# Moving the order of matmuls in the even groups of a decay mix with a routed low-rank layer

## What is computed

```python
ekv_t, ek_t = exp(min(f, 30)) * f, exp(min(f, 30))
# forward and backward over time: a = a * decay + ekv_t ; b = b * decay + ek_t
num = nf + nb - ekv + exp(min(u + f, 30)) * f
den = df + db - ek + exp(min(u + f, 30))
y = sigmoid(x) * num / max(den, 1e-8) * (0.8 + 0.2 * tf)
```

```python
h = silu(y @ rw1.T + rb1)                      # 64 hidden
logits = (h @ rw2.T + rb2)[:, :16] + gates     # top 2, softmax of the two -> coeff
xa = einsum('ni,eri->ner', y, A)               # 256 low-rank sums for a token
out = x + y @ W.T + bias + einsum('ner,eor->no', xa * coeff[:, :, None], B)
```

## Time and profile before

| | |
|---|---|
| median of 3 runs | 720.68 us (720.63 to 720.79) |
| the profiled execution: its time, its span | 720.62 us, 718.8 us |
| PE busy | 597.5 us (83%) |
| PEld busy | 486.8 us (68%) |
| DVE busy | 528.0 us (73%) |
| ACT busy | 349.3 us (49%) |
| POOL busy | 352.2 us (49%) |
| DMA | 74.22 MB, mean 103 GB/s |

### The profile page before, as it was taken

The page is one execution under the profiler, slowest core; times in us unless marked ns, Lnnn a source line. Parts: engine busy times, 40 slices in busy tenths (PEclk is TensorE's granted clock), DMA queues, the critical chain, the costliest instruction groups (busy, mean ns, idle before and its releaser), DMA issues.

```text
span 718.8 us, 6928 instructions
## 1 busy us (share of the span) xinstructions
PE 597.5 (83%) x2626; PEld 486.8 (68%) x2626; DVE 528.0 (73%) x547; ACT 349.3 (49%) x401; POOL 352.2 (49%) x164
## 2 busy tenths in 40 slices
PE   0005342498999999999999999999999999999998
PEld 0003231386888688868886888778887888888886
DVE  7999999799788979796979796979698713021302
ACT  4777876845574556435664565356735420002000
POOL 1789988744754575356536553655464511000100
PEclk9999665599999999999999999999999999999999
DMA  5324442313350435041613261226214310231031
GB/s 181 117 86 143 141 142 88 118 59 117 127 167 30 146 103 191 29 147 59 224 41 120 86 208 56 74 104 209 83 50 138 95 55 1 88 110 38 0 89 73
DMA packets 30865, 74.22 MB, mean 103 GB/s; under 512 B 4464, under 2 KB 4592, under 8 KB 30832
## 3 DMA queue, kind: packets, MB, share of 16 engines
q1 hardware_dynamic: 30832, 73.79, 30.8%
HBM read 57.00 MB, written 16.78 MB: 103 GB/s over the span
## 4 chain that ended last, share of the span: by engine, by line
PE 59%; DVE 16%; POOL 16%; issue 6%; ACT 2%; DMA 0%; DVEq 0%; SPq 0%; POOLq 0%; ACTq 0%
PE acc L707 18%; PE acc L708 18%; PE acc L709 18%; POOL mix L461 5%; DVE mix L534 4%; DVE yr L560 3%; POOL kv L451 3%; POOL yr L456 3%; POOL y_lo L465 2%; POOL wx_lo L471 2%; DVE mix L539 2%; DVE xo L567 2%; PE acc L719 2%; PE acc L718 2%; ACT y_hi L314 1%
## 5 line engine op out<-in xcount | busy, mean ns | idle before, releaser
L707 PE MATMUL acc<-y_hi,wa_hi 128*128 128x512 f32 x640 | 257.3, 402 | 10.5 <-DVE xo L567 10.5
L708 PE MATMUL acc<-y_lo,wa_hi 128*128 128x512 f32 x640 | 253.5, 396 | 0.0
L709 PE MATMUL acc<-y_hi,wa_lo 128*128 128x512 f32 x640 | 253.2, 396 | 0.0
L707 PEld LDWEIGHTS acc<-y_hi,wa_hi 128*128 128x128 f32 x640 | 123.0, 192 | 43.6 <-DVE xo L567 18.2
L709 PEld LDWEIGHTS acc<-y_hi,wa_lo 128*128 128x128 f32 x640 | 122.7, 192 | 26.4
L708 PEld LDWEIGHTS acc<-y_lo,wa_hi 128*128 128x128 f32 x640 | 123.0, 192 | 24.9
L461 POOL TENSOR_TENSOR mix<-mix,kv 128x1024 f32<-128x1024 f32 x31 | 74.1, 2390 | 90.6 <-DVE mix L518 73.7
L718 PE MATMUL acc<-y_hi,wr 128*128 128x512 f32 x64 | 27.3, 426 | 99.3 <-POOL wa_lo L439 63.6
L567 DVE SCALAR_TENSOR_TENSOR xo<-acc,bias_sb,xo 128x512 f32<-128x512 f32 x64 | 46.7, 736 | 76.5 <-PE acc L709 76.4
L465 POOL TENSOR_TENSOR y_lo<-yr,y_hi 128x1024 fp32r<-128x1024 f32 x32 | 76.6, 2395 | 49.9 <-ACT y_hi L314 49.9
L471 POOL TENSOR_TENSOR wx_lo<-xa,wx_hi 128x512 fp32r<-128x512 f32 x16 | 20.4, 1298 | 152.6 <-ACT wx_hi L373 152.6
(11 more groups left out here) (85 smaller groups left out, 767.4 us busy)
## 6 DMA issues: line engine op xcount, KB each, us to landing
kv<-f_cm SPq DMA_DIRECT2D x32, 512.0 KB, 3.3
yr<-x_cm SPq DMA_DIRECT2D x32, 512.0 KB, 3.3
xo<-x_cm SPq DMA_DIRECT2D x64, 256.0 KB, 4.0
out<-xo SPq DMA_DIRECT2D x64, 256.0 KB, 3.5
xo<-w_base SPq DMA_DIRECT2D x5, 512.0 KB, 3.5
xa<-w_base SPq DMA_DIRECT2D x3, 512.0 KB, 4.3
xa<-w_router_a SPq DMA_DIRECT2D x2, 480.0 KB, 3.4
xo<-w_expert SPq DMA_DIRECT2D x1, 512.0 KB, 3.8
```

Of the source, the lines that this page charges most:

```text
L707: nc.tensor.matmul(out_ap, wh, yh, start=start, stop=False)
L708: nc.tensor.matmul(out_ap, wh, yl, start=False, stop=False)
L709: return nc.tensor.matmul(out_ap, wl, yh, start=False, stop=stop)
```

## The change

In the even groups, TensorE goes over the channel blocks in the outermost loop: for each kc the router, both low-rank sums, and, three units behind (LAG), base block 0. Base block 1 comes ahead of the logits, base block 2 between logits and spreads, behind a wait for the first low-rank copy, and the last three units of block 0 behind the spreads. `bank_in` waits for the evacuation that frees a bank, just ahead of the first matmul into it. Group 0's waits for weights are joined into one for each kc. Odd groups keep their order; only the way in which the waits are written is new. No instruction is added or removed but waits, and no other engine's order is touched.

```diff
--- before.py
+++ after.py
@@ -760,46 +760,62 @@
                 if G % 2 == 0:
                     pe.wait_ge(lo_ready, G // 2 * CB + kc + 1)
 
+            def bank_in(G, n):
+                if G:
+                    pe.wait_ge(evacuated, (G - 1) * CB + 4 + n)
+
             for G in range(GROUPS):
-                if G == 0:
+                LAG = 3
+                if G % 2 == 0:
                     for kc in range(CB):
                         unit_in(G, kc)
-                        pe.wait_ge(w_lo_ready, router_a_chunk[kc] + 1)
+                        if G == 0:
+                            pe.wait_ge(w_lo_ready, max(router_a_chunk[kc], base_chunk[kc]) + 1)
+                        if kc == 0:
+                            bank_in(G, 0)
                         hid(G, kc)
-                        low_rank(G, 0, kc)
-                        low_rank(G, 1, kc)
-                        pe.wait_ge(w_lo_ready, base_chunk[kc] + 1)
+                        for a in range(2):
+                            if kc == 0:
+                                bank_in(G, 1 + a)
+                            low_rank(G, a, kc)
+                        if kc >= LAG:
+                            if kc == LAG:
+                                bank_in(G, 3)
+                            base(G, 0, kc - LAG)
+                    bank_in(G, 4)
+                    for kc in range(CB):
+                        base(G, 1, kc)
+                    if G == 0:
+                        pe.wait_ge(late_in, 16 * 7)
+                    logits(G)
+                    pe.wait_ge(xa_copied, 2 * G + 1)
+                    for kc in range(CB):
+                        base(G, 2, kc)
+                    pe.wait_ge(xa_copied, 2 * G + 2)
+                    for a in range(2):
+                        spread(G, a)
+                    for kc in range(CB - LAG, CB):
                         base(G, 0, kc)
-                    pe.wait_ge(late_in, 16 * 7)
                 else:
-                    first = 5 if G % 2 == 0 else CB
-                    pe.wait_ge(evacuated, (G - 1) * CB + 4)
-                    for kc in range(first):
-                        unit_in(G, kc)
+                    bank_in(G, 0)
+                    for kc in range(CB):
                         hid(G, kc)
                     for a in range(2):
-                        pe.wait_ge(evacuated, (G - 1) * CB + 5 + a)
-                        for kc in range(first):
+                        bank_in(G, 1 + a)
+                        for kc in range(CB):
                             low_rank(G, a, kc)
-                    for kc in range(first, CB):
-                        unit_in(G, kc)
-                        hid(G, kc)
-                    for a in range(2):
-                        for kc in range(first, CB):
-                            low_rank(G, a, kc)
-                    pe.wait_ge(evacuated, (G - 1) * CB + 7)
+                    bank_in(G, 3)
                     for kc in range(CB):
                         base(G, 0, kc)
-                logits(G)
-                if G:
-                    pe.wait_ge(evacuated, G * CB)
-                for kc in range(CB):
-                    base(G, 1, kc)
-                pe.wait_ge(xa_copied, 2 * G + 2)
-                for a in range(2):
-                    spread(G, a)
-                for kc in range(CB):
-                    base(G, 2, kc)
+                    logits(G)
+                    bank_in(G, 4)
+                    for kc in range(CB):
+                        base(G, 1, kc)
+                    pe.wait_ge(xa_copied, 2 * G + 2)
+                    for a in range(2):
+                        spread(G, a)
+                    for kc in range(CB):
+                        base(G, 2, kc)
                 for a in range(2):
                     pe.wait_ge(wx_ready, 2 * G + a + 1)
                     for kc in range(2):
```

## The result

The changed kernel took 732.24 us (median of 4 runs, 730.4 to 734.37), the kernel before 720.68 (720.63 to 720.79). The ratio is 1.0161, 95% interval 1.0129 to 1.0193: slower by 11.6 us. The runs of before lie within 0.2 us, those of the changed kernel within 4. The profiled execution took 730.4 us, its span is 728.6: 9.8 us over the one of before.

A forecast was written before the change was run, and what follows sets the result against it. Bound: a loop of TensorE's work from block 5 to logits plus DVE's stretch from logits to evacuations. 0.6 (group 0) + 0.5 (clock, block 2) + 2 x 3.41 (late logits) + 3 x 0.5 (clock, block 5) = 9.4: 730.1 us, range 726.0 to 733.5.

The forecast's parts named there:

- rival A: The forecast: late logits are paid for in groups 2 and 4, with some clock falls, 727.5 to 732.5 us; chance 0.65.
- B: Rival: every gap brings TensorE's clock to half, each at its full price, 732.5 to 735.5 us; chance 0.16.
- full price: Most that half clock costs behind a gap: 1.45 us ahead of block 5, 2.75 us ahead of group 0's block 2.
- the lateness of group 0: In group 0, spreads, DVE's second weighing, the evacuation and block 5 come 0.6 us later.
- Logits 15 matmuls later: Groups 2 and 4: DVE's routing and evacuations move with the logits, costing 3.41 us each, 6.8 together; group 6 costs 0.
- The late router sum: Group 2: sum read at 289.1 instead of 283.92, hidden vector still 1.9 us ahead of logits; cost 0.
- covering the 4.67 us: Group 0: block 1 fills TensorE's 4.67 us of idleness before logits; DVE gains nothing, 3.3 us of waiting ahead of block 5.
- The clock: Half clock at new gaps: 0.5 us ahead of group 0's block 2, 0.5 at each of three ahead of block 5.
- the 0.5 us ahead of block 2: Group 0: clock cost of the 2.85 us gap ahead of block 2, between 0 and 2.75 us, taken as 0.5.
- C: Rival: DVE's 19.26 us from routing to evacuation shrink by 1 to 2 in groups 2 and 4, 724.0 to 727.5; chance 0.12.
- D: Rival: the first evacuation follows TensorE's results, not routing; groups 2 and 4 lose nothing, 718.0 us; chance 0.04.
- E: Rival: DVE's waiting and idleness absorb all but 0.4 of the 3.41 us, nothing measurable, 720 to 722 us; chance 0.03.

The follow-up runs named there:

- e12: The changed kernel with its four new gaps filled by 55 matmuls that nobody needs: 727.48 us.
- e3: The kernel before with only the logits of groups 2, 4 and 6 moved 15 matmuls later, inside base block 1: 731.06 us.
- e7: The changed kernel with logits of groups 2, 4 and 6 back behind 88 matmuls and spreads 24 matmuls behind them: 727.47 us.
- e6: The changed kernel with units of blocks 3 and 4 moved ahead of block 5, four in even groups and two in odd ones: 720.04 us.
- e9: e1 with the last three units of group 0's block 0 right behind its logits, ahead of the wait for the low-rank copy: 721.72 us.
- e1: The new order in group 0 alone, groups 1 to 7 as in the kernel before: 724.43 us.
- e2: The new order in groups 2, 4 and 6 alone, the other groups as in the kernel before: 728.94 us.
- e5: The kernel before with two more units of blocks 3 and 4 (12 matmuls) moved ahead of block 5 in every group: 708.62 us.
- e10: e9 with units of blocks 3 and 4 moved ahead of block 5, two in groups 1 to 7, all six in group 0: 709.01 us.
- e11: e10 with logits six matmuls earlier in groups 1 to 7 and spreads 24 matmuls behind them: 708.34 us.

## Why the prediction was right

It said 730.1 us, 726.0 to 733.5, slower; 732.24 were measured. The main mechanism, rival A's, is what the traces show. Part of B holds as well: the clock went to half around all four new gaps, though in the median not at B's full price. That the shortest execution took 730.4 us, next to the forecast, is luck: the median is 2.1 us over it, since the lateness of group 0 was put 0.5 us too high and the clock 2.8 too low, and the longest run, 734.37, lies outside the range, in B's.

**Logits 15 matmuls later, 3.41 us in each of groups 2 and 4, nothing in group 6.** Shown. The gap ahead of block 5 is 3.74 us, DVE's stretch kept its length to 0.03 us, group 6's reserve shrank by 3.41; e12 has 6.9 us for lateness in all, where 6.8 were counted for these groups; and e3 moves block 5 by 3.44 us with the position of the logits alone.

**The late router sum at no cost.** Right for this kernel: read at 289.2 where 289.1 was said, wait for logits 0.83 where 0.8 was said. e7 and e6 show how near it was: with logits at their old place it costs 2.6 us a group, with the gaps filled it bounds the kernel.

**Group 0: covering the 4.67 us gains nothing.** Right, routing began at 143.28. The 0.6 us of lateness was too much, and the gap ahead of block 5 is 2.69 us, not 3.3. In the changed kernel block 5 comes 1.70 us late (166.88 against 165.18), but nearly all of that is block 2 at half clock. In e12, where spreads came at 151.79 as said and the next scan behind the weighing 0.75 us late, block 5 is only 0.1 late (group 1's logits at 218.70 against 218.62): an operation of DVE in between was shorter by 0.65, see below.

**The clock.** The mechanism was right and the size was off: 2.0 us were counted (0.5 and three times 0.5), and the medians give 4.8, single runs 2.9 to 6.9. The term that failed first is the 0.5 us ahead of block 2, taken as small because its gap was thought to be the shortest. It is the dearest in the medians, since nothing hides the slow matmuls there and DVE waits for the spreads behind them: e9, whose gap there is 1.21 us where e1 has 3.93, is 2.7 us faster than e1. Behind block 5 of group 0 the price changes most. By how much later than block 5 the logits of group 1 are, it is 0.03 us in the profile of the changed kernel, 1.75 in that of e1 and 1.95 in that of e9; 0.5 was counted and 1.45 given as the most. Behind block 5 of groups 2 and 4, e2 has 728.94 - 720.67 - 6.82 = 1.5 us for both, 0.7 each against 0.5. The slow block 5 hid there, as said: the second gap, 1.19 us, is gone in these groups, and so the statement that it would stay was wrong. Mostly for this reason the waits for evacuations came to 15.7 us and not to about 20.

**The Trainium skill's rule.** By the Trainium skill (TensorE: Matmul & The Clock Gate, HAM oscillation) bursts of matmuls between long enough waits are throttled again at every one of them. The profiled execution agrees: the clock went to half around each of its four new gaps (3.03, 2.69, 3.74 and 3.73 us). The full price of the four, by the prediction's own bounds, is 2.75 + 3 x 1.45 = 7.1 us. The median paid 4.8, the shortest run 2.9, the longest 6.9. The prediction calls the full price 3.9 us more than it counts; its own terms give 7.1 - 2.0 = 5.1.

C, D and E are out: nothing in the 19 us shrank, and the evacuation did not follow TensorE's results.

## What to carry to other kernels

When an engine's work is handed over in a loop (matmuls, then a fixed stretch of another engine, then matmuls that need it), count what stands ahead of the handover and what stands beside the other engine's stretch; moving work from the first to the second is worth the gap that it closes (e5 moved 2.7 us a group, closed gaps of 1.7 to 1.9 and gained 12.0 in all), and the other way costs its length where no reserve takes it up (3.41 us in groups 2 and 4, nothing in group 6), though the work stays the same. It ends where the other engine becomes the bound (e10, e11). Filling an idle stretch ahead of a handover gains nothing if the receiver wasn't waiting (group 0). A gap in TensorE's work can cost more than its length, by the half clock behind it, where nothing hides what comes behind it (2.7 us between e1 and e9): put real work there, or split the work around it.

## What the runs showed of the hardware

Behind group 0's logits, the granted clock was at half in or behind every gap of 2.1 us or more that the profiles show: 2.10 and 2.17 us in e6, 2.20 and 2.21 in e3, 2.69 to 3.74 in the changed kernel, 2.88 in e10, 3.93 in e1. Around most gaps of 1.2 to 1.8 us it stayed full, but not around all: e6 has it at half behind its gap of 2.10 us, which ended at 346.27, and e7 behind one of 1.45 us, which ended at 447.82, though not behind one of 1.46 us at 296.10. The stretches are first of e6, then of e7 (columns as in the earlier trace rows):

```profile
346.30:347.00 0.70, 0.70 (x3) 0.61 (x4) 0.70 (x2) 0.70 (x1) 0.70 (x1) 1.00 0.00 0
347.20:350.40 3.20, 3.20 (x9) 2.52 (x8) 3.20 (x3) 0.30 (x1) 3.12 (x2) 0.50 0.92 264
```

```profile
447.90:449.20 1.30, 1.30 (x10) 1.23 (x11) 1.30 (x1) 1.28 (x2) 1.22 (x2) 1.00 0.00 0
449.60:452.80 3.20, 3.20 (x9) 2.47 (x8) 2.96 (x22) 1.21 (x4) 1.23 (x1) 0.50 0.30 91
```

Where it fell, and for how long, changed from gap to gap and from run to run. With the four gaps filled, the scatter of 4 us went down to 0.1 (e12), so it came from them.

DVE's scaling of 128 x 1024 elements (line 518) is longer beside GpSimd. The timelines of DVE in the kernel before and in e12, and of POOL in e12:

```profile
158.13 1.54 DVE L518 TENSOR_SCALAR mix<-mix,delta_g 128x1024 f32<-128x1024 f32 x1
```

```profile
158.88 0.89 DVE L518 TENSOR_SCALAR mix<-mix,delta_g 128x1024 f32<-128x1024 f32 x1
```

```profile
156.82 2.41 POOL L465 TENSOR_TENSOR y_lo<-yr,y_hi 128x1024 fp32r<-128x1024 f32 x1
```

Where GpSimd is idle it takes 0.74 us; in groups 1 to 5 of the kernel before, beside the same GpSimd operation, 1.53 to 1.56. In both kernels it ends 0.54 us behind the end of the GpSimd operation (159.67 and 159.13 in the kernel before, 159.77 and 159.23 in e12), though it starts 0.75 us later in e12, which gave group 0 its 0.65 us back. That it waits for GpSimd is read from these ends; no run took it apart.
